# Linear attention with a soft-tree layer on one core: other PSUM banks for the fills, and another order in each turn

## The reference

```python
# attention, 16 heads of 64, causal and linear
Q = phi(xn @ Wq + bq); K = phi(xn @ Wk + bk); V = xn @ Wv + bv      # phi(t) = elu(t) + 1
KV = KV + outer(k_i, v_i); Ks = Ks + k_i                           # running over tokens
out_i = (q_i @ KV) / (q_i . Ks + 1e-6);  attn = out @ Wo + bo
# soft tree of depth 8
gate = sigmoid((xn @ tree_Wq.T) @ routers.T)                       # 255 nodes
leaf_prob = product of gates along each of 256 paths
tree = (leaf_prob @ leaf_values) @ Wout_w.T + Wout_b
result = x + attn + tree
```

## Time and profile before

| | us |
|---|---|
| median of 3 runs | 1363.02 |
| profiled execution | 1362.36 |
| its span, first to last instruction | 1360.7 |
| TensorE matmul busy | 1279.9 (94%) |
| VectorE busy | 806.9 (59%) |
| ScalarE busy | 619.5 (46%) |
| GpSimd busy | 373.7 (27%) |

### The profile page before, as it was taken

One profiled execution on the slowest core, in us unless ns is written; L12 is line 12 of the kernel. 1 busy time (PEld: TensorE's weight loads), 2 busy tenths in 40 slices (PEclk: granted clock), 3 DMA queues, 4 the chain that ended last, 5 costly groups with the idle time before them and its releaser, 6 DMA issues.

```text
span 1360.7 us, 49950 instructions
## 1 busy us (share of the span) xinstructions
PE 1279.9 (94%) x22173; PEld 1117.7 (82%) x22173; DVE 806.9 (59%) x2186; ACT 619.5 (46%) x1135; POOL 373.7 (27%) x590
## 2 busy tenths in 40 slices
PE   5899999999999999899999999999999999999987
PEld 5789788897978879788897978879788787878976
DVE  4664756656476564765657566574765647566462
ACT  4453544535355253453535345353553535445351
POOL 3514132141322314133141321413223141321410
PEclk9899999999999999999999999999999999999998
DMA  6000000010000100001010000100001000000000
GB/s 209 18 3 17 18 5 31 2 33 3 10 26 2 33 3 18 18 2 33 3 28 7 10 26 3 33 3 17 19 2 33 2 19 17 10 10 3 18 2 17
DMA packets 21603, 26.00 MB, mean 19 GB/s; under 512 B 1025, under 2 KB 19728, under 8 KB 21392
## 3 DMA queue, kind: packets, MB, share of 16 engines
q1 hardware_dynamic: 21392, 22.82, 5.2%
HBM read 14.43 MB, written 8.39 MB: 17 GB/s over the span
## 4 chain that ended last, share of the span: by engine, by line
PE 77%; ACT 12%; DVE 6%; issue 3%; DMA 1%; SPq 0%; DVEq 0%
PE w_pair L638 24%; PE s_pair L650 17%; PE s_pair L638 11%; PE kv_pair L723 6%; PE s_pair L708 5%; ACT ex L405 5%; PE o_pair L762 5%; PE o_pair L748 5%; ACT ex L408 4%; DVE qT L520 3%; PE o_pair L690 3%; DVE oT L536 2%; ACT k_tok L420 2%; PE w_pair L685 2%; ACT ffn_tok L413 1%
## 5 line engine op out<-in xcount | busy, mean ns | idle before, releaser
L328 POOL TENSOR_SCALAR_AFFINE_SELECT aT<-aT 64x512 f32<-64x512 f32 x256 | 167.7, 655 | 918.5 <-ACT aT L434 910.2
L405 ACT ACTIVATE ex<-w_pair,neg_bias 128x512 f32<-128x512 f32 x256 | 176.3, 689 | 197.0 <-PE w_pair L638 194.3
L638 PE MATMUL w_pair<-xnT,wk 128*128 128x512 f32 x768 | 214.1, 414 | 1.1 <-ACT k_tok L421 0.8
L638 PE MATMUL s_pair<-wv,xnT 128*128 128x512 f32 x744 | 200.5, 408 | 0.0
L638 PE MATMUL w_pair<-xnT,wq 128*128 128x512 f32 x768 | 197.6, 393 | 0.2 <-DVE wq L241 0.2
L650 PE MATMUL s_pair<-wo,oT 128*128 128x256 f32 x1536 | 191.1, 281 | 0.0
L577 DVE TENSOR_TENSOR snaps<-kv_pair,snaps 128x65 f32<-128x65 f32 x768 | 173.4, 226 | 26.4
L650 PEld LDWEIGHTS s_pair<-wo,oT 128*128 128x128 f32 x1536 | 185.6, 189 | 0.0
L638 PEld LDWEIGHTS w_pair<-xnT,wq 128*128 128x128 f32 x768 | 144.6, 189 | 32.6 <-DVE wq L241 0.6
L434 ACT ACTIVATE aT<-s_pair 128x512 f32<-128x512 f32 x128 | 76.4, 597 | 200.5 <-PE s_pair L708 200.5
L408 ACT ACTIVATE ex<-ex 128x512 f32<-128x512 f32 x256 | 161.8, 632 | 8.1
(11 more groups left out here) (102 smaller groups left out, 1773.1 us busy)
## 6 DMA issues: line engine op xcount, KB each, us to landing
x_in<-in_L_attn_x_dram SPq DMA_DIRECT2D x16, 512.0 KB, 3.9
out_dram<-y_buf SPq DMA_DIRECT2D x32, 256.0 KB, 2.2
stage<-in_L_attn_Wv_dram SPq DMA_DIRECT2D x2, 512.0 KB, 7.9
stage<-in_L_attn_Wk_dram SPq DMA_DIRECT2D x2, 512.0 KB, 9.7
stage<-in_L_attn_Wq_dram SPq DMA_DIRECT2D x2, 512.0 KB, 10.9
stage<-in_L_attn_Wo_dram SPq DMA_DIRECT2D x2, 512.0 KB, 9.2
bv_all<-in_L_attn_bv_dram SPq DMA_DIRECT2D x1, 512.0 KB, 8.6
ffn_tok<-in_L_ffn_Wq_dram SPq DMA_DIRECT2D x1, 256.0 KB
```

What stands on the lines that cost most here:

```text
L328: pool.affine_select(out=part, in_=part, compare_op=ALU.is_ge, fill=0.0, base=0, pattern=[[0, 2 * CH], [1, D]], channel_multiplier=-1).the ...
L405: act.activation(ex[:, slot], psum_of(name), ACT.Relu, scale=-1.0, bias=neg_bias[:, col:col + 1])\
L638: last = pe.matmul(dst, l, r, start=i == 0, stop=i == len(steps) - 1)
```

## The change

Three things change. The table gives other banks: queries are filled in S0 instead of W1, output transposes in W1 instead of O0, the transposed inputs in O0 and O1, and the leaves and some of the value chunks in O1. Its order changes: the fills in the output banks come right behind the queries, then those in S1, then the key transposes, and the output transposes last; in the last turn of a block (p = 7) the output transposes stay ahead of the rows y, which need them. And the keys are copied to `k_tok` by one instruction instead of two halves; the outer products wait once for it, where before they waited for the first half, and in the middle for the second. The output transposes, no longer in an output bank, keep their wait for the division.

```diff
@@ unit_fills
+    own = [(("oT", p, g), W1)]
     fills = []
     if ahead:
-        fills += [(("K", ahead[1], ahead[0]), W0), (("Q", ahead[1], ahead[0]), W1)]
-    fills.append((("oT", p, g), O0))
+        fills += [(("K", ahead[1], ahead[0]), W0), (("Q", ahead[1], ahead[0]), S0)]
     if p == 0:
-        fills += [(("V1", 0, g), S0), (("V1", 1, g), S1)]
+        fills += [(("V1", 0, g), O1), (("V1", 1, g), S1)]
     if p == 1:
-        fills += [(("V1", 2, g), S0)]
+        fills += [(("V1", 2, g), S1)]
     if p == 2:
-        fills += [(("V1", 3, g), S0)]
         if more:
-            fills += [(("xT", 0, g + 1), S1), (("xT", 1, g + 1), O1)]
+            fills += [(("xT", 0, g + 1), O0), (("xT", 1, g + 1), O1)]
+        fills += [(("V1", 3, g), S1)]
     if p in (3, 4):
-        fills += [(("leaf", p - 3, g), S0)]
+        fills += [(("leaf", p - 3, g), O1)]
         if more:
             fills += [(("V0", p - 3, g + 1), S1)]
     if p in (5, 6) and more:
-        fills += [(("V0", p - 3, g + 1), S0), (("gate", p - 5, g + 1), S1)]
-    if p == 7:
-        fills += [(("y", 0, g), S0), (("y", 1, g), S1)]
+        fills += [(("V0", p - 3, g + 1), O1), (("gate", p - 5, g + 1), S1)]
+    if p == PAIRS - 1:
+        fills += own + [(("y", 0, g), O1), (("y", 1, g), S1)]
     if ahead:
         fills.append((("kT", ahead[1], ahead[0]), W0))
+    if p < PAIRS - 1:
+        fills += own
     return fills
@@ copy_keys
-                half = CH // 2 * P
-                to = k_tok[:, :, :].rearrange("p c n -> p (c n)")
-                act.activation(to[:, 0:half], psum_of(name)[:, 0:half], ACT.Copy).then_inc(keys_begun, 1)
-                act.activation(to[:, half:], psum_of(name)[:, half:], ACT.Copy).then_inc(drained[bank_of[name]], 1)
+                act.activation(k_tok[:, :, :].rearrange("p c n -> p (c n)"), psum_of(name), ACT.Copy)\
+                   .then_inc(drained[bank_of[name]], 1)
@@ outer_products
-                    if t == 0:
-                        pe.wait_ge(keys_begun, n + 1)
-                    if t == CH // 2:
-                        until_drained(("kT", p, n // PAIRS))
@@ outer_products_when_ready
+                until_drained(("kT", p, g))
                 outer_products(n)
@@ fills on TensorE
-                    if bank in (O0, O1):
+                    if bank in (O0, O1) or kind == "oT":
                         pe.wait_ge(o_normed, n + 1)
```

More of the change, by code:

```diff
@@ L217, in attention_and_tree_layer @@
         drained = [sem(f"bank{i}_drained") for i in range(6)]
-        keys_begun = sem("keys_begun")
         hi_ready = sem("hi_ready")
```

## The result

The changed kernel took 1379.99 us (median of four runs, 1371.4 to 1383.4) against 1362.97 of the kernel before on the same chip: a ratio of 1.0112, with a 95% interval of 1.0065 to 1.0159. It is slower by 15 to 17 us, or 1.1%, where the prediction had it faster by 47. Its profiled execution took 1383.44 us, 21.1 more than that of before.

A forecast was written before the change was run, and what follows sets the result against it. The prediction took TensorE, busy 94% of the span, as the bound, with gains only from its idle and overlong groups. 2.95 us a block times 15 (44.3) plus 2.5 gave 46.8 us: 1316 us, range 1303 to 1333.

The forecast's parts named there:

- The terms of the sum: Gains forecast for each of a block's eight turns, totalling 2.95 us a block, 44.3 us over 15 blocks.
- The signs: L748's 1.5 us waits shrink to about 0.4; v_aug wait before pair 4's outer products; leafT waits replace oT's low part.
- Turn 2: Output's low part goes last in VectorE's queue, so state products start earlier; scores at 648.82 instead of 649.76, 0.94 us gained.
- late key phi: Turn 1: the key's phi comes 0.53 us late, so the key transposes wait 0.12 to 0.15 us.
- Turn 7: Only the whole key copy matters: key transposes to scores take 2.01 us instead of 1.86, 0.15 us lost.
- the rival of the division: Early fills in O0 and O1 wait for VectorE's division of the last outputs (o_tok): slower, 1383 us; 3%.
- that of the pacing copy: ScalarE's whole key copy, as long as two halves and starting late, paces every turn: smaller gain, 1335 us; 14%.
- the wait for the output's low part is replaced by one for the leaf's: Turns 3 and 4, before L748: the leaf's low part ends earlier, scores at 584.09 instead of 584.45, 0.36 us gained each.
- to the good: the stalls inside L762: Stalls within the chunk products, listed with patternless slow-clock stretches as possible extra gain; clock kept up some 5 us, with the rest 1303.
- 3% for slower: Chance given to the changed kernel measuring slower than before, against 2% for same and 95% for faster.
- forecast 2.5 gained: Last block, without transposed input or gates: 0.33 + 0.45 + 0.33, and 1.41 in turn 6, gives 2.5 us.
- one without a pattern: Slow-clock stretch near 1226, clock 0.57 over 4 us, 3.4 of them at 1.2 GHz; counted among stretches that fall without a pattern.

The follow-up runs named there:

- the kernel with the two waits exchanged: The changed kernel with the waits for O0 and O1 ahead of from_state in the other order, so the first matmul carries O1: 1329.3 us, ratio 0.9764.
- both with a wait for each bank: Changed kernel and kernel before, each output bank waited for by the first matmul that writes it: 1324.3 us (ratio 0.9736) and 1354.2 us (0.9958).
- each bank with spare waits: The changed kernel with each output bank's wait at its first matmul, plus never-held wait instructions in the K, Q, V and gate fills: 1316.7 us, ratio 0.9677.

## Why the prediction was wrong

**The terms of the sum held.** From one turn's K to the next, medians of each turn, before minus the kernel with the two waits exchanged (in after itself the stalls sit in the medians of turns 3 and 4):

| turn p | 0 | 1 | 2 | 3 | 4 | 5 | 6 | 7 | block |
|---|---|---|---|---|---|---|---|---|---|
| forecast | 0.33 | 0.45 | 0.94 | 0.36 | 0.36 | 0.33 | 0.33 | -0.15 | 2.95 |
| measured | 0.24 | 0.36 | 0.74 | 0.40 | 0.43 | 0.26 | 0.21 | -0.17 | 2.47 |

Over 15 blocks 37 us in place of 44. The signs came too, and in after itself. Turn 2 of the same block as the earlier trace rows, in the timeline (start us, us, engine line):

```profile
657.24 1.28 DVE L512 TENSOR_TENSOR xnT<-o_pair,xnT 128x512 fp32r<-128x512 f32 x2
657.26 0.60 PE L685 MATMUL w_pair<-ident,kT 128*128 128x128 f32 x4
...
657.90 0.60 ACT L420 ACTIVATE k_tok<-w_pair 128x512 f32<-128x512 f32 x1 [0.39 <-PE w_pair L685]
...
658.43 0.68 DVE L529 TENSOR_TENSOR v_aug<-s_pair,bv_all 128x512 f32<-128x512 f32 x1
...
658.62 0.24 PE L744 MATMUL o_pair<-state,qT 64*64 64x65 f32 x1 [0.32 <-issue]
...
659.37 0.69 PE L719 MATMUL kv_pair<-v_aug,k_tok 64*64 64x65 f32 x32 [0.29 <-DVE v_aug L529]
...
660.11 0.30 PE L708 MATMUL s_pair<-qT,kT 64*64 64x64 f32 x5
```

K is 652.10 here and was 641.05. The low parts end at 658.52 and L744 follows by 0.10, as forecast: K + 6.52 against 6.50. Its wait of 1.50 us is one of 0.32. The values end at 659.11 = K + 7.01 (forecast 7.00). But the outer products follow by 0.26 and not by 0.05, for two separate wait instructions stand before them (the last starts at 659.26); this is the 0.20 that turn 2 fell short. Turn 1 has its late key phi: the wait of the weight load for it (6.9 us, 13 times, above; ten of them in turn 1) is 0.4 us each, but most of that lies under the product before. The key transposes start 0.38 us behind the last value product in the median turn 1, 0.24 in before: 0.14 late, forecast 0.12 to 0.15. Turn 7, against the earlier trace rows:

```profile
628.33 0.60 PE L685 MATMUL w_pair<-ident,kT 128*128 128x128 f32 x4
...
629.61 0.69 PE L719 MATMUL kv_pair<-v_aug,k_tok 64*64 64x65 f32 x32 [0.29 <-ACT k_tok L420]
...
630.36 0.66 PE L708 MATMUL s_pair<-qT,kT 64*64 64x64 f32 x32
```

2.03 us from key transposes to scores; forecast 2.01. The whole copy took 595 ns on average over 128 (forecast 597). The fills in the output banks hardly wait for the division: TensorE's waits for o_tok are two in front of the output transposes (2.5 us), now in W1, and one of 0.2 us of the weight load in front of a transposed input. So the rival of the division is refuted, and that of the pacing copy as well.

**What failed is the sum itself: a term was missing.** The prediction took TensorE's instructions as always at hand, and so it took one wait for another at no cost: in turns 3 and 4 "the wait for the output's low part is replaced by one for the leaf's". For the moment at which L744 may start that is right. But the first wait is on O0, carried by the product, and the second on O1, in the separate instruction, and that exchange holds back the next packet. Its only word on the matter is "to the good: the stalls inside L762", four of them and 4.0 us, which I had left unnamed. They were the same fetch, caught in time nearly always because before's late bank happened to be the one that the product waits for by itself. The rival that came true, on the slower side, was not among those listed, so 3% for slower was far too little. The bill, in us of the profiled executions: dependencies -37 in 15 blocks; stalls +53.6 (59.1 - 5.5); clock 0.992 to 0.989, so 30.4 us at the lower level in place of 21.8, at half the cost +4. From the last block's first key fill to the end it took 78.0 us in before and 78.9 in after, 5.3 of them stalls: about -4 of dependencies (forecast 2.5 gained). The sum is +17, the measurement +21.1; some 4 us are not placed. From after to the exchanged waits: stalls -40.3, clock 0.989 to 0.999 another -14, together -54; measured -53.0. The clock's part is an estimate and the agreement in part luck: 5 of the 14 us are a stretch of 10.2 us at the lower level near the end (from 1356), which before and after have and this one profile has not, and the same kernel's other three executions, at 0.994 to 0.995, took 1327.3 to 1331.9 us, no longer than the profiled one.

**The clock.** It falls behind long stalls. After one of 2.3 us at 640.2 (start and end us, length, busy time and instructions of PE, PEld, DVE, ACT and POOL, PEclk, DMA share, GB/s):

```profile
640.00:642.00 2.00, 0.24 (x18) 0.29 (x9) 1.85 (x8) 0.43 (x1) 1.37 (x2) 1.00 0.28 91
642.00:644.00 2.00, 1.49 (x4) 1.17 (x4) 1.42 (x5) 0.00 (x0) 0.06 (x1) 0.69 0.00 0
644.00:646.00 2.00, 2.00 (x6) 1.63 (x5) 0.00 (x0) 0.87 (x2) 0.00 (x0) 0.50 0.00 0
```

TensorE is nearly idle for 2 us, and then has the clock at 0.50, its level of 1.2 GHz, while it is fully busy. The fall of before near 1226 has such a stall ahead of it. The chain there:

```profile
1223.49 0.35 PE o_pair L762 x22
1223.84 1.74 issue
1225.58 0.44 PE o_pair L762 x10
```

The prediction counted that fall as one without a pattern. In after there are four, at 444.8, 642.7, 810.0 and 922.6, each of 3.4 us and each right behind a stall of 2.1 to 2.5 us. Over all eleven profiles that were read, away from the first and last 60 us, there are 24 such falls, every one within 1.6 us of the end of a stall of 1.9 us or more. Four kernels (after with the waits exchanged, both with a wait for each bank, and each bank with spare waits) have one such stall between them, and no fall. After the stall at 758 the clock stayed at 1.00, so not each stall does it.

**What stays open.** The rule in the sequencer isn't settled. In turns 3 to 5 a late packet starts about 1 us behind the end of the separate wait, and a hold in that instruction delays it, while a hold in a product's own wait doesn't. But in the same fills other separate waits are passed earlier, unheld, and let nothing go, and in the long rows y packets go out with no wait near. Whether a count, a queue or the state of the sequencer decides, no run here tells apart.

## What to carry to other kernels

Idle that is put down to "issue", in the middle of a group without a wait, at instructions a fixed number apart, is instruction fetch: count TensorE's instructions in program order and look where the instruction queue's packets start. Before dense stretches of small products, let the condition that comes last be carried by the product that needs it, and only conditions that are long met stand in separate waits; here that was worth 50 us of 1380 by itself, and hid a gain of 30. When a stall in the profile of before has no name, find it before counting it "to the good": a change that moves the idle around it can multiply it.

## What was not expected of the hardware

- A block of 256 instructions (one 16 KB packet) was in use 2.2 to 2.9 us after its packet had started, in over 200 stalls of ten profiles, and TensorE runs 256 instructions of 64-wide products in 2.3 us: a fetch that starts late can't keep up.
- The order in which the same four conditions are written decides which of them goes into a separate instruction: +47 us in before, -51 in after.
- Waits written twice (implied by an earlier one) cost nothing: they are not in the program.
